# A graph layer and a 64-expert feed-forward layer on one core: node sums in rows, shared-expert pieces and the base addition earlier in the run

## The chip, the cores and the metric

The program runs on one core of a Trainium2 chip. The metric is the device time of one execution in microseconds (us), smaller is better. TensorE (PE), VectorE (DVE), ScalarE (ACT), GpSimd (POOL) and SyncE (SP) work side by side and meet at semaphores. Here SP issues the loads of weights, and POOL issues all gathers and scatters between the on-chip memory and DRAM.

## The reference, cut to what matters

```python
# x (625, 512); src, dst: 5000 edges in both directions and 625 loops, sorted by dst
h0  = layernorm(x)
agg = segment_sum(h0[src], dst, 625)
h   = (1 + eps) * h0 + agg
h   = relu(batch_norm(h @ W1 + b1)); h = relu(batch_norm(h @ W2 + b2))
x   = x + h0 + h
xn  = layernorm(x)
gate = the 6 best of softmax(xn @ Wr) over 64 experts, rescaled to sum 1
out = x + xn + sum over 2 shared experts of ffn(xn) + sum over 64 experts of ffn_e(xn) * gate[:, e]
# ffn: (silu(x @ Wg) * (x @ Wu)) @ Wd, all matrices 512 x 512, float32
```

## The kernel before, in words

**The graph part.** The 625 nodes are T = 5 blocks of P = 125. The sum over edges is a product with the matrix A that counts edges from each source node to each destination node. A is made block by block of destinations: each block has GB = 5 groups of 25 destinations, and each group has U = 5 chunks of edges. For each group DVE makes two arrays of ones and zeros, 125x625 each, by comparing a constant with a column: `one_s` (source) and `one_m` (destination and source block) in `group_onehots` (L697 to L702). PE multiplies them (`visit`, L1097, five matmuls) and ACT copies the block's product from PSUM into `aT` (`at_copy`, L484 and L486). DVE adds (1 + eps) to the diagonal of `aT` (`at_diag`, L761). Then PE aggregates (`aggregate`, L1110): for each of 4 column quarters and 5 source blocks one matmul with `h0` as the stationary operand and `aT` as the moving one, 20 matmuls of 125 columns in float32. What comes out is h transposed, and ACT copies it to `hT` (L497). On PE the order is visits(0), visits(1), aggregate(0), visits(2), aggregate(1), and so on. Two products with weights and batch norms follow (L1172 and L1185), then layer norm and routing, until about 165 us.

**The expert part.** It is one loop over j = 0 to 63 (L1425 to L1467 on PE). The experts are sorted by how many rows they have; the table ROWS says how many rows are worked for the j-th: 96 for j up to 5, 64, 60, 56 and 52 for j = 6 to 46, 96 and 80 for j = 47 to 62. Below, j = 6 to 46 are the light rounds. One round of PE does, in this order: the gate product of j, the transposes of the hidden rows of j-1 (`ident,hs`), the transposes of the gathered rows of j+1 (`ident,xg`, L1355), a small product for the slots of j+3 (L1270), the up product of j, in some rounds a piece of the shared experts, and the down product of j-1. Where an expert has 96 rows, up comes right after gate (`gate_and_up`, L1379). X(j) is the time at which PE transposes the rows of j.

**The pieces.** The two shared experts are 26 pieces: per expert 8 for gate and up (L1325 and L1335 each half of one) and 5 for down (L1346, 8 matmuls, added to `x_sb` by DVE). Three are done ahead of the loop or at j = 0, and 23 are spread evenly over j = 6 to 46 by the table `unit_at` (L310 to L313).

**POOL's order.** POOL executes gather(j), then scatter(j-5), for j = 0 to 68. A gather reads rows of `x_tab` into one of three `xg` buffers (L424). A scatter adds expert j's rows in `ysb` to `out` in DRAM (L436). Scatters are one behind another: each waits until the one before has landed, and there are three `ysb` buffers, which ACT fills (L623). After scatter 47 (`BASE_AFTER`) POOL issues the base: two transfers that add `x_sb` to `out` (L446). They wait for all ten down pieces and for scatter 47. Scatter 48 waits for the base.

**The ring.** SP loads each expert's three matrices (1 MB each) in the order of use into 13 slots. A load waits for the last product that read its slot, and the core's other transfers share the DMA engines with them.

Of the kernel before, what the change touches and what calls it, by code (L numbers as in the profile page):

```python
# [21 lines left out]
def gnn_moe_kernel(nc, x_in, src_in, dst_in, eps_in, W1, b1, g1, be1, W2, b2, g2, be2,  # L22
# [42 lines left out]
    BASE_AFTER = 47  # L65
    NY = 3
    PRE = 3 * 16
# [4 lines left out]
    with ctx:  # L72
# [58 lines left out]
        iota_m = m("iota_m", [P, P], i16)  # L131
# [33 lines left out]
        aT = [rAT.place(f"aT{i}", [P, T, P], f32) for i in range(2)]  # L165
# [43 lines left out]
        ring = [rOh.place(f"ring{i}", [128, KD, 512], f32) for i in range(8)]  # L209
# [31 lines left out]
        def sem(name):  # L241
# [14 lines left out]
        s_vecT, s_sm, s_vis, s_atc, s_at, s_h0, s_nrm, s_xs = (sem(n) for n in (  # L256
            "vectors_T", "group_onehots", "group_visited", "aT_copied", "aT_ready", "h0_ready", "norm_ready", "extra_round"))
        s_agg, s_hT, s_hpad = (sem(n) for n in ("aggregated", "hT_ready", "hT_padded"))
# [56 lines left out]
        assert max(unit_at) < BASE_AFTER  # L315

# [4 lines left out]
        def _(sp):  # L321
# [54 lines left out]
        def _(pool):  # L376
# [13 lines left out]
            g.iota(iota_m[:], pattern=[[1000, T], [1, G]], base=1000, channel_multiplier=0).then_inc(s_cst, 1)  # L390
# [83 lines left out]
        def _(act):  # L474
# [20 lines left out]
            def agg_copy(b):  # L495
                act.wait_ge(s_agg, b + 1)
                sc.activation(hT[:, :, b * P:(b + 1) * P],  # L497
                              ps[:, 4 + b % 2, 0:KD * P].rearrange("p (k n) -> p k n", k=KD), ACT.Copy).then_inc(s_hT, 1)

            block_copy(0)  # L500
# [3 lines left out]
            for t in range(T):  # L504
                sc.activation(h0[:, t, :], x_sb[:, t, :], ACT.Identity, bias=negm[:, t:t + 1],
                              scale=rstd[0:P, t:t + 1]).then_inc(s_h0, 1)
            act.wait_ge(s_pre, PRE)
            block_copy(1)
            for b in range(2, T):
                agg_copy(b - 2)  # L510
                block_copy(b)
            agg_copy(T - 2)
            agg_copy(T - 1)
            act.wait_ge(s_round, 1)
            more_rounds = act.value_load(rounds_i[0:1, 0:1], min_val=0, max_val=XROUNDS)
            with act.If(more_rounds > 0):
                with act.Fori(0, more_rounds) as o:
                    for b in range(T):
                        act.wait_ge(s_vis, o * NG + (NG + GB * (b + 1)))
                        act.wait_ge(s_agg, o * T + (T + b))  # L520
                        at_copy(b, 0, 0)
# [9 lines left out]
            act.wait_ge(s_at, T)  # L531
# [125 lines left out]
        def _(dve):  # L657
# [39 lines left out]
            def group_onehots(g, slot):  # L697
                c = slice(g * U, (g + 1) * U)
                for one, iota, col in ((one_s, iota_s, col_s), (one_m, iota_m, col_m)):
                    last = v.tensor_tensor(one[slot][:], iota[:].unsqueeze(1).broadcast_to([P, U, P]),  # L700
                                           col[:, c].unsqueeze(2).broadcast_to([P, U, P]), ALU.is_equal)
                last.then_inc(s_sm, 1)  # L702

            def block_onehots(b, first=0, end=GB):
                for g in range(b * GB + first, b * GB + end):
                    if g >= NSM:
                        dve.wait_ge(s_vis, g - NSM + 1)
                    group_onehots(g, g % NSM)

            dve.wait_ge(s_col, 1)  # L710
            link(columns())
# [45 lines left out]
            def at_diag(b):  # L757

                dve.wait_ge(s_atc, 2 * b + 2)
                sl = aT[b % 2][:, b, :]  # L760
                v.scalar_tensor_tensor(sl, ident[0:P, 0:P], eps1[:], sl, ALU.mult, ALU.add).then_inc(s_at, 1)  # L761

            dve.wait_ge(s_pre, PRE)
            v.memset(hT[:, :, N:NP], 0.0).then_inc(s_hpad, 1)
            for b in range(1, T):
                block_onehots(b, 0, 2)
                at_diag(b - 1)
                block_onehots(b, 2, GB)
            at_diag(T - 1)
            dve.wait_ge(s_round, 1)  # L770
            more_rounds = dve.value_load(rounds_i[0:1, 0:1], min_val=0, max_val=XROUNDS)
            with dve.If(more_rounds > 0):
                with dve.Fori(0, more_rounds) as o:
# [6 lines left out]
                    for b in range(T):  # L780
                        dve.wait_ge(s_vis, o * NG + (NG + GB * b))
                        for i in range(GB):
                            group_onehots(b * GB + i, i)
                        dve.wait_ge(s_agg, o * T + (T + b + 1))
                        block = hT[:, :, b * P:(b + 1) * P]
                        v.tensor_tensor(block, block, ps[:, 4, 0:KD * P].rearrange("p (k n) -> p k n", k=KD),
                                        ALU.add).then_inc(s_hT, 1)
# [295 lines left out]
        def _(pe):  # L1083
# [26 lines left out]
            def aggregate(from_aT, bank):  # L1110
                for d in range(KD):
                    for s in range(T):
                        last = t_.matmul(ps[:, bank, d * P:(d + 1) * P], h0[:, s, d * 128:(d + 1) * 128],
                                         from_aT[:, s, :], start=(s == 0), stop=(s == T - 1))
                last.then_inc(s_agg, 1)

            def block_aggregate(b):
                pe.wait_ge(s_at, b + 1)
                if b == 0:
                    pe.wait_ge(s_h0, T)  # L1120
                if b >= 2:
                    pe.wait_ge(s_hT, b - 1)
                aggregate(aT[b % 2], 4 + b % 2)
# [391 lines left out]
```

## Time and profile before

| | |
|---|---|
| Median of 3 runs | 772.82 us (771.66 to 773.99) |
| The profiled execution | 773.9 us, span 772.2 us |
| Mean granted TensorE clock | 0.987 |
| Busy: PE, DVE, ACT, POOL | 714.7, 260.2, 196.8, 171.7 us |
| Moved by DMA | 236.34 MB, 306 GB/s on average |

The durations used below are those of the profiled execution. Its span leaves out 1.7 us at the ends. PE is busy 93% of the span, so first one asks which stretches of PE could be shorter, and then where PE stands idle.

### The profile page before, as it was taken

The numbers are of one execution on the slowest core, as the hardware profiler recorded it, in microseconds if no ns is written. First come the engines' busy times: TensorE is split into PE (matmuls) and PEld (weight loads), VectorE is DVE, ScalarE is ACT, GpSimd is POOL, SyncE is SP. The second block draws the span as 40 slices with busy tenths as digits, with TensorE's granted clock in tenths as the row PEclk, the third lists the DMA queues.
The fourth block names the chain that finished last, engine by engine and source line by source line (L and its number), as shares of the span: only waits on it lengthen the run. The fifth ranks groups of instructions, "written<-read, shape, count | busy, mean of one in ns | idle before, by whom it ended". The sixth has DMA issues, their size and how long they took to land. (4 is left out here: it accounts for less than half of the span.)

```text
span 772.2 us, 17458 instructions
## 1 busy us (share of the span) xinstructions
PE 714.7 (93%) x7096; PEld 485.1 (63%) x7096; DVE 260.2 (34%) x788; ACT 196.8 (25%) x497; POOL 171.7 (22%) x157
## 2 busy tenths in 40 slices
PE   2599999879999999999999999999999996999991
PEld 2597777556776666555566666655557774777760
DVE  7982624976112442222212212122332221222110
ACT  1222422311332222221122222212112331333331
POOL 4000000011222222232232213222333312222222
PEclk9999999999999999999999999999999998999997
DMA  8970020434999999999999999999999999999951
GB/s 259 407 296 3 0 109 21 169 113 158 371 359 349 350 379 392 395 385 391 373 390 386 380 388 384 393 384 386 382 388 380 374 358 344 373 371 371 371 137 24
DMA packets 57264, 236.34 MB, mean 306 GB/s; under 512 B 6171, under 2 KB 6335, under 8 KB 40286
## 3 DMA queue, kind: packets, MB, share of 16 engines
q1 hardware_dynamic: 46004, 211.33, 71.4%
q0 software_dynamic: 10144, 20.56, 11.4%
q10 hardware_dynamic: 1034, 3.30, 1.1%
q8 instruction: 59, 0.97, 0.5%
q14 instruction: 23, 0.19, 0.1%
HBM read 222.32 MB, written 12.83 MB: 305 GB/s over the span
## 5 line engine op out<-in xcount | busy, mean ns | idle before, releaser
L1362 PE MATMUL ps<-ring,xT 128*64 128x256 f32 x1296 | 153.6, 382 | 0.0
L424 POOL DMA_INDIRECT xg<-x_tab,idx_sb x64 | 68.9, 1076 | 368.0 <-DVE idx_sb L937 201.9
L436 POOL DMA_INDIRECT out<-ysb,idx_sb x64 | 92.5, 1445 | 217.5 <-issue 180.2
L1362 PEld LDWEIGHTS ps<-ring,xT 128*64 128x64 f32 x1296 | 91.1, 137 | 44.3 <-issue 1.6
L930 DVE TENSOR_REDUCE gates<-ps 128x1 f32<-128x3 f32 (+1 forms) x62 | 10.0, 162 | 285.8 <-PE ps L1270 277.4
L623 ACT ACTIVATE ysb<-ps 64x256 f32<-64x256 f32 x64 | 24.2, 378 | 260.6 <-PE ps L1362 211.3
L1362 PE MATMUL ps<-ring,hTj 128*64 128x256 f32 x624 | 76.3, 387 | 0.0
L1362 PE MATMUL ps<-w,xT 128*64 128x256 f32 x608 | 71.9, 381 | 0.0
L898 DVE TENSOR_TENSOR onehot<-iotaAB,slotv 125x640 bf16<-125x640 f32 (+1 forms) x64 | 67.3, 1051 | 1.4 <-PE ps L1278 1.0
L1362 PEld LDWEIGHTS ps<-ring,hTj 128*64 128x64 f32 x624 | 42.5, 138 | 30.5 <-issue 12.6
L1362 PEld LDWEIGHTS ps<-w,xT 128*64 128x64 f32 x608 | 42.5, 137 | 20.4
L994 DVE SCALAR_TENSOR_TENSOR hs<-hs,gates,ps 128x256 f32<-128x256 f32 x64 | 30.7, 480 | 59.8 <-PE ps L1362 41.9
L613 ACT ACTIVATE hs<-ps 128x256 f32<-128x256 f32 (+1 forms) x64 | 26.9, 421 | 91.3 <-PE ps L1369 52.1
L1362 PE MATMUL ps<-w,hTj 128*64 128x256 f32 x320 | 38.6, 383 | 2.1 <-ACT hTj L617 2.1
L1325 PE MATMUL ps<-xnT,sw 128*128 128x312 f32 (+1 forms) x128 | 37.9, 438 | 0.4 <-ACT lg L566 0.4
L1346 PE MATMUL ps<-sw,hsT 128*125 128x512 f32 x80 | 37.0, 605 | 0.0
L1335 PE MATMUL ps<-xnT,sw 128*128 128x312 f32 (+1 forms) x128 | 36.5, 427 | 0.0
L1355 PE MATMUL ps<-ident,xg 96*128 96x96 f32 (+5 forms) x256 | 30.1, 239 | 6.8 <-DMA xg<-x_tab,idx_sb 6.8
L1172 PE MATMUL ps<-hT,w 128*128 128x313 f32 x128 | 34.1, 427 | 1.7 <-issue 1.7
L1185 PE MATMUL ps<-r,w 128*128 128x313 f32 x128 | 34.1, 426 | 0.0
L1362 PEld LDWEIGHTS ps<-w,hTj 128*64 128x64 f32 x320 | 22.0, 137 | 16.2 <-issue 6.7
L1355 PEld LDWEIGHTS ps<-ident,xg 96*128 96x128 f32 (+5 forms) x256 | 22.6, 140 | 14.5 <-DMA xg<-x_tab,idx_sb 7.5
(237 smaller groups left out, 820.9 us busy)
## 6 DMA issues: line engine op xcount, KB each, us to landing
ring<-in_L_ffn_Wg SPq DMA_DIRECT2D x41, 1024.0 KB
ring<-in_L_ffn_Wu SPq DMA_DIRECT2D x40, 1024.0 KB
ring<-in_L_ffn_Wd SPq DMA_DIRECT2D x39, 1024.0 KB
w<-in_L_ffn_Wd SPq DMA_DIRECT2D x20, 1024.0 KB
w<-in_L_ffn_Wg SPq DMA_DIRECT2D x19, 1024.0 KB
w<-in_L_ffn_Wu SPq DMA_DIRECT2D x19, 1024.0 KB
ring_x<-in_L_ffn_Wu SPq DMA_DIRECT2D x5, 1024.0 KB
ring_x<-in_L_ffn_Wd SPq DMA_DIRECT2D x5, 1024.0 KB
```

Source lines behind the costliest of these rows:

```text
L424: g.indirect_dma_start(out=xg[j % NX][0:ROWS[j], :], out_offset=None, in_=x_tab, in_offset=bass.IndirectOffsetOnAxis(ap=idx_sb[0:ROWS[j], ...
L436: g.indirect_dma_start(out=out, out_offset=bass.IndirectOffsetOnAxis(ap=idx_sb[0:ROWS[j], j:j + 1].bitcast(u32), axis=0), in_=ysb[j % NY][ ...
L613: sc.activation(o, i, ACT.Silu).then_inc(s_silu, 1)
L898: v.tensor_tensor(onehot[e % 2][:].rearrange("p t a c -> p t (a c)")[:, :, 0:n], iotaAB[0:P, :, :].rearrange("p a c -> p (a c)")[:, 0:n].u ...
L994: last = v.scalar_tensor_tensor(o, o, ga, u, ALU.mult, ALU.mult)
L1172: last = t_.matmul(ps[:, q + h, 0:HALF], w1[buf][:, k, col:col + 128], halves(hT, k)[h], start=(k == 0), stop=(k == KD - 1))
L1185: last = t_.matmul(ps[:, q + h, 0:HALF], w2[k // KD][:, k % KD, col:col + 128], halves(r1, k)[h], start=(k == 0), stop=(k == KH - 1))
L1325: last = t_.matmul(ps[:, 5, 0:PART[h]], sw[0][:, k, f * 128:(f + 1) * 128], xnT[:, k, c0:c0 + PART[h]], start=(k == 0), stop=(k == KD - 1))
L1335: last = t_.matmul(ps[:, 6, 0:PART[h]], sw[1][:, k, f * 128:(f + 1) * 128], xnT[:, k, c0:c0 + PART[h]], start=(k == 0), stop=(k == KD - 1))
L1346: last = t_.matmul(ps[0:P, 5, :], hsT[:, k, t * P:(t + 1) * P], sw[2][:, k, :], start=(k == 0), stop=(k == KD - 1))
L1355: last = t_.transpose(ps[:, 4, k * rows:(k + 1) * rows], xg[h][0:rows, k * 128:(k + 1) * 128], ident[0:rows, 0:rows])
L1362: last = t_.matmul(ps[h * BIG:(h + 1) * BIG, bank, 0:AW], big(k), w[:, k, h * AW:(h + 1) * AW], start=(k == 0), stop=(k == KD - 1))
```

## The change

- **Compares.** ACT writes the column of a group out to its full width (`rep`, 125x625 in int16, ten buffers), and DVE compares two 2-byte arrays of full width. This is done for `one_m` in all 25 groups, and for `one_s` in the last five. 30 ACT instructions are added.
- **Aggregation.** It now gives rows: `aT` is the stationary operand and h0 the moving one, 512 columns wide. As `aT` and h0 are read in the type f32r, h0 is split into a rounded part `h0_hi` (5 more ACT instructions) and the rest `h0_lo` (5 subtractions on DVE): 10 matmuls per block in place of 20. DVE adds (1 + eps) h0 on the way out of PSUM (`h_rows`, 125x512, in place of `at_diag`), and PE transposes the rows (4 per block). Block b is aggregated right after its own visits; the transposes come one block later.
- **Last block.** DVE adds it into `hT`, where ACT copied before.
- **Memory.** The new arrays lie where ring slots 4 to 7 are, so SP loads those slots only after `hT` is done.
- **Gate and up** are adjacent for all experts from j = 1.
- **Pieces.** The 23 pieces are spread over j = 6 to 34 (the last is at 33, and runs after X(34)).
- **Base.** It follows scatter 36, and from there on POOL issues gather(j+1) ahead of scatter(j-5), where it was gather(j).

The diff, cut to its core:

```diff
-    BASE_AFTER = 47
+    BASE_AFTER = 36
+    NREP = 10
...
-        free = [j for j in range(FIXED, FIXED + E - LAST - NBIG) if j not in (SPREAD + 4, SPREAD + 5)]
+        free = [j for j in range(FIXED, 35) if j not in (SPREAD + 4, SPREAD + 5)]
...
             for i, (r, j) in enumerate(items):
+                if i == 4:
+                    sp.wait_ge(s_hT, T)
...
             for j in range(E + LAG):
-                if j < E:
+                if j < E and j <= BASE_AFTER + LAG + 1:
                     gather(j)
                 if j >= LAG:
+                    if BASE_AFTER + LAG + 1 < j + 1 < E:
+                        gather(j + 1)
                     scatter(j - LAG)
                 if j == BASE_AFTER + LAG:
                     add_base()
...
+                    sc.activation(rep[n % NREP][:], col[:, g * U:(g + 1) * U].unsqueeze(2).broadcast_to([P, U, P]),
+                                  ACT.Copy).then_inc(s_rep, 1)
...
             for b in range(2, T):
-                agg_copy(b - 2)
+                if b + 1 < T:
+                    spread(b + 1)
                 block_copy(b)
...
+            def h_rows(b):
+                dve.wait_ge(s_agg, b + 1)
...
+                v.scalar_tensor_tensor(hrow[b % 2][:], h0[:, b, :], eps1[:], ps[0:P, 4 + b % 2, :], ALU.mult,
+                                       ALU.add).then_inc(s_hrow, 1)
...
-            def aggregate(from_aT, bank):
-                for d in range(KD):
-                    for s in range(T):
-                        last = t_.matmul(ps[:, bank, d * P:(d + 1) * P], h0[:, s, d * 128:(d + 1) * 128],
-                                         from_aT[:, s, :], start=(s == 0), stop=(s == T - 1))
+            def aggregate(from_aT, bank, done):
+                for s in range(T):
+                    for part in (h0_hi, h0_lo):
+                        last = t_.matmul(ps[0:P, bank, :], from_aT[:, s, :], part[:, s, :],
+                                         start=(s == 0 and part is h0_hi), stop=(s == T - 1 and part is h0_lo))
...
+            block_aggregate(0)
+            block_aggregate(1)
             for b in range(2, T):
-                block_aggregate(b - 2)
+                if b == T - 1:
+                    block_transposes(b - 2)
                 visits(b)
+                block_transposes(b - 1 if b == T - 1 else b - 2)
+                block_aggregate(b)
...
-                both = j >= 1 and CAPS[j] > BIG
+                both = j >= 1
```

**POOL around the base.** A name with `ysb` is a scatter, one with `xg` a gather, one with `x_sb` half of the base. Before:

```order
L436 DMA out<-ysb_149,idx_sb 625x512
L446 DMA out<-x_sb 112x5x512
L446 DMA out<-x_sb 13x5x512
L424 DMA xg_141<-x_tab,idx_sb 80x512
L436 DMA out<-ysb_147,idx_sb 625x512
L424 DMA xg_139<-x_tab,idx_sb 80x512
L436 DMA out<-ysb_148,idx_sb 625x512
```

and in the change, where the first row is scatter 36:

```order
L457 DMA out<-ysb_150,idx_sb 625x512
L467 DMA out<-x_sb 112x5x512
L467 DMA out<-x_sb 13x5x512
L445 DMA xg_142<-x_tab,idx_sb 52x512
L445 DMA xg_143<-x_tab,idx_sb 52x512
L457 DMA out<-ysb_151,idx_sb 625x512
L445 DMA xg_144<-x_tab,idx_sb 52x512
L457 DMA out<-ysb_152,idx_sb 625x512
```

The gathers behind the base are now of 52 rows, gather 42 is still right behind it, and gather 43 has moved ahead of scatter 37.

**ACT in the graph part.** `aT` rows are the copies of a block of A, `rep` rows the spreads, `hT` rows the copies of h transposed. Before, for blocks 3 and 4:

```order
L484 ACTIVATE aT_101<-ps 125x4x5x25
L486 ACTIVATE aT_101<-ps 125x5x25
L497 ACTIVATE hT<-ps 128x4x125
L484 ACTIVATE aT_100<-ps 125x4x5x25
L486 ACTIVATE aT_100<-ps 125x5x25
```

and in the change, from block 2's copies to those of block 3:

```order
L507 ACTIVATE aT_99<-ps 125x4x5x25
L509 ACTIVATE aT_99<-ps 125x5x25
L520 ACTIVATE hT<-ps 128x4x125
L530 ACTIVATE rep_104<-col_s 125x625
L530 ACTIVATE rep_168<-col_m 125x625
L530 ACTIVATE rep_169<-col_s 125x625
L530 ACTIVATE rep_170<-col_m 125x625
L530 ACTIVATE rep_171<-col_s 125x625
L530 ACTIVATE rep_172<-col_m 125x625
L530 ACTIVATE rep_173<-col_s 125x625
L530 ACTIVATE rep_174<-col_m 125x625
L530 ACTIVATE rep_175<-col_s 125x625
```

One more `rep` row follows, and then block 3's copies: all ten spreads of the last block stand ahead of them.

**PE in the light rounds.** A round runs from one `ident,xg` row to the next; `xT` rows are gate or up, `hTj` rows down, and `xnT,sw` rows a piece. Before, one whole round with a gate and up piece, from X(34) to X(35):

```order
L1355 MATMUL ps<-ident,xg_140 128x56 x4
L1270 MATMUL ps<-gsel_89,onehot_174 128x5 x5
L1362 MATMUL ps<-w_0_118,xT_143 64x256 x8
L1325 MATMUL ps<-xnT,sw_165 128x312 x4
L1335 MATMUL ps<-xnT,sw_166 128x312 x4
L1362 MATMUL ps<-w_1_119,hTj 64x256 x8
L1362 MATMUL ps<-w_0_163,xT_142 64x256 x8
L1395 MATMUL ps<-ident,hs_145 128x128 x2
L1355 MATMUL ps<-ident,xg_141 128x56 x4
```

and in the change two rounds, the last piece (`hsT`, a down piece) in the first of them:

```order
L1449 MATMUL ps<-ident,xg_143 128x56 x4
L1364 MATMUL ps<-gsel_88,onehot_188 128x5 x5
L1440 MATMUL ps<-sw_181,hsT 125x512 x4
L1456 MATMUL ps<-w_1_122,hTj 64x256 x8
L1456 MATMUL ps<-w_0_177,xT_145 64x256 x8
L1456 MATMUL ps<-w_1_178,xT_145 64x256 x8
L1493 MATMUL ps<-ident,hs_148 128x128 x2
L1449 MATMUL ps<-ident,xg_144 128x56 x4
L1364 MATMUL ps<-gsel_89,onehot_189 128x5 x5
L1456 MATMUL ps<-ring_x,hTj 64x256 x8
L1456 MATMUL ps<-ring_158,xT_146 64x256 x8
L1456 MATMUL ps<-ring_159,xT_146 64x256 x8
```

Gate and up have come together, and from the second round on, up to j = 46, no round has a piece.

## Rows read from the trace of the kernel before

**Rows 1.** The page: busy time, granted clock in tenths and GB/s in 40 slices.
```profile
PE 714.7 (93%) x7096; PEld 485.1 (63%) x7096; DVE 260.2 (34%) x788; ACT 196.8 (25%) x497; POOL 171.7 (22%) x157
...
GB/s 259 407 296 3 0 109 21 169 113 158 371 359 349 350 379 392 395 385 391 373 390 386 380 388 384 393 384 386 382 388 380 374 358 344 373 371 371 371 137 24
```

**Rows 2.** Timeline of PE, graph part: start us, us, instructions, [idle before <-releaser].
```profile
31.09 7.00 PE L1113 MATMUL ps<-aT,h 125*128 125x125 f32 x40 [0.18 <-issue]
37.92 1.61 PE L1100 MATMUL ps<-one_m,one_s 125*125 125x125 bf16 x25
39.37 4.68 PE L1113 MATMUL ps<-aT,h 125*128 125x125 f32 x40
...
63.71 34.05 PE L1172 MATMUL ps<-hT,w 128*128 128x313 f32 x128 [1.67 <-issue]
```

**Rows 3.** Timeline of DVE, graph part.
```profile
9.16 0.81 DVE L700 TENSOR_TENSOR one_s<-iota_s,col_s 125x625 bf16<-125x625 int16 x1
9.89 0.81 DVE L700 TENSOR_TENSOR one_m<-iota_m,col_m 125x625 bf16<-125x625 int16 x1
...
22.52 0.81 DVE L700 TENSOR_TENSOR one_s<-iota_s,col_s 125x625 bf16<-125x625 int16 x1
...
51.69 0.81 DVE L700 TENSOR_TENSOR one_m<-iota_m,col_m 125x625 bf16<-125x625 int16 x1
```

**Rows 4.** Timeline of ACT, graph part.
```profile
22.34 3.64 ACT L505 ACTIVATE h<-x_sb,negm,rstd 125x512 f32<-125x512 f32 x5 [1.26 <-DVE negm L751]
...
53.09 0.60 ACT L484 ACTIVATE aT<-ps 125x500 f32<-125x500 f32 x1 [2.35 <-PE ps L1100]
53.58 0.27 ACT L486 ACTIVATE aT<-ps 125x125 f32<-125x125 f32 x1
```

**Rows 5.** Groups of instructions by line and shape: busy us, mean ns of one, idle before.
```profile
L952 DVE COPY scratch<-scratch 128x42 f32<-128x42 f32 x1 | 0.2, 185 | 0.0
L952 DVE COPY scratch<-scratch 128x22 f32<-128x22 f32 x1 | 0.2, 178 | 0.0
...
L1346 PE MATMUL ps<-sw,hsT 128*125 128x512 f32 x80 | 37.0, 605 | 0.0
L1016 DVE TENSOR_TENSOR x_sb<-x_sb,ps 125x512 f32<-125x512 f32 x10 | 6.9, 688 | 30.6 <-PE ps L1346 30.6
```

**Rows 6.** Timeline of PE at X(6), X(33), X(34), X(35), X(53) and X(63).
```profile
225.92 0.46 PE L1355 MATMUL ps<-ident,xg 64*128 64x64 f32 x4
...
461.79 0.45 PE L1355 MATMUL ps<-ident,xg 56*128 56x56 f32 x4
...
468.09 0.46 PE L1355 MATMUL ps<-ident,xg 56*128 56x56 f32 x4
...
478.94 0.45 PE L1355 MATMUL ps<-ident,xg 56*128 56x56 f32 x4
...
645.75 0.79 PE L1355 MATMUL ps<-ident,xg 80*128 80x80 f32 x4 [6.55 <-DMA xg<-x_tab,idx_sb]
...
743.28 0.45 PE L1355 MATMUL ps<-ident,xg 52*128 52x52 f32 x4
```

**Rows 7.** Timeline of POOL around the base: scatter 47, base, gather 53, scatter 48.
```profile
616.25 1.46 POOL L436 DMA_INDIRECT out<-ysb,idx_sb  x1 [2.47 <-issue]
625.65 2.53 POOL L446 DMA_DIRECT2D out<-x_sb  x2 [7.94 <-DMA out<-ysb,idx_sb]
628.48 1.02 POOL L424 DMA_INDIRECT xg<-x_tab,idx_sb  x1 [0.30 <-issue]
645.60 1.52 POOL L436 DMA_INDIRECT out<-ysb,idx_sb  x1 [16.10 <-DMA out<-x_sb]
```

**Rows 8.** Timeline of POOL: scatters in the light rounds, the last after X(33).
```profile
353.98 1.45 POOL L436 DMA_INDIRECT out<-ysb,idx_sb  x1 [5.46 <-issue]
...
362.07 1.45 POOL L436 DMA_INDIRECT out<-ysb,idx_sb  x1 [3.46 <-issue]
...
464.84 1.45 POOL L436 DMA_INDIRECT out<-ysb,idx_sb  x1 [0.30 <-issue]
```

**Rows 9.** Waits: who waited for what, us in total, times, longest.
```profile
ACT ysb L623 <- DMA out<-ysb,idx_sb: 43.2, 10, 7.2
```

**Rows 10.** Windows: length, busy us (x) of PE, PEld, DVE, ACT, POOL, granted clock, DMA share, GB/s.
```profile
300.00:400.00 100.00, 100.00 (x750) 58.88 (x746) 21.50 (x62) 23.00 (x62) 28.23 (x23) 1.00 1.03 387
```

More of the change, by code:

```diff
@@ L164, in gnn_moe_kernel @@
         ring_x = rH0.place("ring_x", [128, KD, 512], f32)
-        aT = [rAT.place(f"aT{i}", [P, T, P], f32) for i in range(2)]
+        aT = [rAT.place(f"aT{i}", [P, T, P], f32r) for i in range(2)]
+        iota_m = rAT.place("iota_m", [P, U, P], i16)
+        hrow = [rAT.place(f"hrow{i}", [P, D], f32) for i in range(2)]
+        rep = [rAT.place("rep0", [P, U, P], i16)]
         rAT.rewind()
@@ L208, in gnn_moe_kernel @@
         cntS = rWin.place("cntS", [128, E], f32)
-        ring = [rOh.place(f"ring{i}", [128, KD, 512], f32) for i in range(8)]
+        ring = [rOh.place(f"ring{i}", [128, KD, 512], f32) for i in range(4)]
+        upper = rOh.at
+        ring += [rOh.place(f"ring{4 + i}", [128, KD, 512], f32) for i in range(4)]
+        past = rOh.at
+        rOh.at = upper
+        h0_hi = rOh.place("h0_hi", [P, T, D], f32r)
+        h0_lo = rOh.place("h0_lo", [P, T, D], f32r)
+        rep += [rOh.place(f"rep{i}", [P, U, P], i16) for i in range(1, NREP)]
+        assert rOh.at <= past
+        rOh.at = past
         w2 = [rOh.place(f"w2_{i}", [128, KD, 512], f32) for i in range(2)]
@@ L315, in gnn_moe_kernel @@
         assert max(unit_at) < BASE_AFTER
+        BOTH_FROM = NG - GB
+        spreads = [(g, c) for g in range(NG) for c in (("s", "m") if g >= BOTH_FROM else ("m",))]
+        spread_at = {gc: n for n, gc in enumerate(spreads)}
         block = ctx.enter_context(nc.Block())
@@ L493, in block_copy, with hT_copy, spread @@
                 at_copy(b, b % 2, 2 * (b % 2))
-            def agg_copy(b):
-                act.wait_ge(s_agg, b + 1)
+            def hT_copy(b):
+                act.wait_ge(s_hrT, b + 1)
                 sc.activation(hT[:, :, b * P:(b + 1) * P],
-                              ps[:, 4 + b % 2, 0:KD * P].rearrange("p (k n) -> p k n", k=KD), ACT.Copy).then_inc(s_hT, 1)
+                              ps[:, 6 + b % 2, 0:KD * P].rearrange("p (k n) -> p k n", k=KD), ACT.Copy).then_inc(s_hT, 1)
+            def spread(b):
+                for n, (g, c) in enumerate(spreads):
+                    if g // GB != b:
+                        continue
+                    if n >= NREP:
+                        act.wait_ge(s_sm, spreads[n - NREP][0] + 1)
+                    col = col_m if c == "m" else col_s
+                    sc.activation(rep[n % NREP][:], col[:, g * U:(g + 1) * U].unsqueeze(2).broadcast_to([P, U, P]),
+                                  ACT.Copy).then_inc(s_rep, 1)
+            act.wait_ge(s_colm, 1)
+            spread(0)
+            spread(1)
             block_copy(0)
@@ L695, in columns, with group_onehots @@
                 return v.tensor_tensor(col_m[:], ps[0:P, 6, 256:256 + NV], grp_of[:], ALU.subtract)
[L697 removed]
+            def group_onehots(g, slot, spread):
                 c = slice(g * U, (g + 1) * U)
[L699 to L701 removed]
+                if spread and g >= BOTH_FROM:
+                    v.tensor_tensor(one_s[slot][:], iota_s[:].unsqueeze(1).broadcast_to([P, U, P]),
+                                    rep[spread_at[g, "s"] % NREP][:], ALU.is_equal)
+                else:
+                    v.tensor_tensor(one_s[slot][:], iota_s[:].unsqueeze(1).broadcast_to([P, U, P]),
+                                    col_s[:, c].unsqueeze(2).broadcast_to([P, U, P]), ALU.is_equal)
+                if spread:
+                    last = v.tensor_tensor(one_m[slot][:], iota_m[:], rep[spread_at[g, "m"] % NREP][:], ALU.is_equal)
+                else:
+                    last = v.tensor_tensor(one_m[slot][:], iota_m[:], col_m[:, c].unsqueeze(2).broadcast_to([P, U, P]),
+                                           ALU.is_equal)
                 last.then_inc(s_sm, 1)
@@ L755, in _ @@
             link(v.tensor_scalar(eps1[:], ps[0:P, 7, 300:301], 1.0, None, ALU.add))
[L757 to L761, printed above, removed]
-            dve.wait_ge(s_pre, PRE)
[L764 to L769, printed above, removed]
+            def h_rows(b):
+                dve.wait_ge(s_agg, b + 1)
+                if b >= 2:
+                    dve.wait_ge(s_hrT, b - 1)
+                v.scalar_tensor_tensor(hrow[b % 2][:], h0[:, b, :], eps1[:], ps[0:P, 4 + b % 2, :], ALU.mult,
+                                       ALU.add).then_inc(s_hrow, 1)
+            block_onehots(1)
+            for t in range(T):
+                dve.wait_ge(s_hi, t + 1)
+                dve.wait_ge(s_h0, t + 1)
+                v.tensor_tensor(h0_lo[:, t, :], h0[:, t, :], h0_hi[:, t, :].bitcast(f32), ALU.subtract).then_inc(s_lo, 1)
+            block_onehots(2, 0, 4)
+            h_rows(0)
+            block_onehots(2, 4, GB)
+            block_onehots(3, 0, 2)
+            h_rows(1)
+            block_onehots(3, 2, GB)
+            h_rows(2)
+            block_onehots(4, 0, 4)
+            h_rows(3)
+            block_onehots(4, 4, GB)
+            dve.wait_ge(s_pre, PRE)
+            v.memset(hT[:, :, (T - 1) * P:NP], 0.0).then_inc(s_hadd, 1)
+            h_rows(T - 1)
             dve.wait_ge(s_round, 1)
```

103 lines of the change are left out of this document (69 added, 34 removed).

## The prediction

> **What bounds the kernel now.** I read the page first. PE is busy 714.7 of 772.2 us, while DMA runs at 359 to 396 GB/s in nearly every slice from 190 us on [rows 1]: two resources are close to full side by side. So the question for each stretch is which of the two gives the pace, and whether a shift of PE work makes the other one late. Then the timelines. In the graph part PE waits for the compares of DVE, one after another without a gap, and the first weight product starts at 63.71 us [rows 2, 3]. In the expert part between 300 and 400 us PE is busy 100% with the clock at 1.00 and 387 GB/s [rows 10]. PE's only long idle time there is before X(53), 6.55 us for a gather [rows 6].
>
> Of this kernel's measurement, about 0.3% (2.3 us) can be told from no change. The profiled execution took 773.9 us, 1.1 above the median of 772.8; I sum against 773.9 and take 1.1 off at the end.
>
> **The graph part.** Prices first.
> - A compare is issued every 0.72 us (9.16 to 9.89) [rows 3]. With two full 2-byte inputs its price isn't in the trace. Upper end: 0.72, nothing gained. Lower end: DVE's cheapest rate per element here, 7 ns for 20 elements (185 - 178 ns) [rows 5], so 625 cost 0.22 us. I take 0.45, the middle, as no row is nearer to either end. The Trainium skill, page "VectorE: DVE Perf Modes", section "The perf-mode tier table", says that a two-input operation on 16-bit data in SBUF runs at twice the rate of a float32 one; by it a compare would take about 0.37 us, an estimate from the page, and the graph part would end at most 1 us earlier.
> - A matmul of aggregation is 512 columns in a rounding type. Upper end: the 80 records of the 512-column float32 product are 37.0 us, two records each, so 0.93 us [rows 5]. Lower end: bf16, 1.61 us for 25 matmuls of 125 columns [rows 2], so 0.26 us for 512. I take 0.25, as a type that rounds its operand is nearer to bf16; 10 of them are 2.5 us against half of 9.15, 4.6 us, or 4.68 for 40 records, for a block now [rows 2]. The Trainium skill, page "FP8 and Floating Point Precision", section "TensorE Precision Notes", gives four passes for true float32 and a reduced-precision read of the same bytes; no row of this trace shows that read, and with four passes a block would cost 9.3 us.
> - A spread on ACT, one input of 625: a scaling of 512 is issued every 0.71 us (3.64 / 5, with overlap) [rows 4]; I take 0.65.
> - `h_rows` and the last add on DVE: 0.69 us like the add out of PSUM [rows 5]. A subtraction for `h0_lo`: 0.6.
>
> The path, block by block. DVE starts at 9.16 [rows 3]; with a wait for the first spread it is 9.9. Block 0 takes 5 x (0.72 + 0.45) = 5.8, to 15.7. The statistics between blocks 0 and 1 keep their 6.1 us (9.16 + 10 x 0.72 = 16.4 to 22.52) [rows 3]; block 1 is done at 27.7. ACT scales h0 twice, 10 x 0.71 from 21.7, to 28.8; `h0_lo` is done at 30.7. Then groups 10 to 19 (11.7 us) and three `h_rows` take DVE to 44.3. Here a new wait comes: **ACT has all ten spreads of the last block ahead of block 3's copies.** They can start only as their buffers come free, from group 10's compare on, and end at 46.8. So block 3's copy, for which PE is ready at about 44.2, ends at 47.7, its aggregation at 50.2, `h_rows` at 51.0, and the last group's compares at 51.9 (this last one is at 52.5 now, so DVE's gain is nearly gone). Visit 0.5, copy 0.9 (0.60 and 0.27) [rows 4], aggregation 2.5, `h_rows` 0.7, transposes 0.6 and add 0.7 lead to 57.8; with the 1.0 from there to the first weight product, it starts at 58.8 instead of 63.7. **-4.9 us.** What gives most of it is the end of the chain: the last two aggregations, 9.15 us [rows 2], are now one of 2.5. PE stands idle for some 3 us before block 3's copy. Bounds: -8 (no wait for the spreads, compares 0.37) to +1 (compares 0.72, and a clock that falls in the gaps). The ring loads that must wait for `hT` are issued at 58 and are used after 165: nothing.
>
> **The pieces.** Between X(34) and X(35) a round with a gate and up piece takes 478.94 - 468.09 = 10.85 us, and the one before, without a piece, 6.30 [rows 6]. So a gate and up piece is 4.55, and a down piece 37.0 / 10 = 3.7, with its hand-over 3.78. By the tables, 11 gate and up and 5 down pieces lie between X(6) and X(35) now, and 13 and 10 after the change. So X(35) comes 2 x 4.55 + 5 x 3.78 = **28.0 us later**, and what is left behind X(35) is 28.0 us shorter on PE alone. If PE were the only bound, that is nothing. DMA says otherwise: 12 rounds without a piece take PE 75.6 us; in these the ring wants 3.15 MB an expert, and gather, scatter and base more. So the light rounds run at what the transfers give.
>
> **The scatters.** A scatter follows the landing of the one before. In the light rounds they are issued 362.07 - 353.98 = 8.1 us apart [rows 8], while PE's rounds there average 8.7 with pieces (253.0 / 29 between X(6) and X(35)) [rows 6]; ACT waits ten times, up to 7.2 us, for a `ysb` buffer whose scatter isn't landed [rows 9]. With rounds of 6.3 PE outruns them. Scatter 30 is issued 3.05 after X(33) (464.84 - 461.79) [rows 6, 8], so scatter 32 at X(35)+3.05 and scatter 36 at X(35)+3.05+4 x 8.1 = +35.4. The base is issued 625.65 - 616.25 = 9.4 later [rows 7], +44.8. The gather behind it lets PE start 645.75 - 625.65 = 20.1 after the base [rows 6, 7]: X(42) = X(35)+64.9. PE's own pace is 7 x 6.3 = 44.1. **Stall +20.8 us**, where the stall now, before X(53), is 6.55 and with the rest of that round 7.4 over its neighbours: **-7.4**. The gather that runs ahead doesn't help at 42: gather 42 is itself behind the base.
>
> After the stall scatter 37 starts only when the base has landed, 20 after it, and PE is two scatters ahead. The third `ysb` buffer lets one round through, and the next four light ones go at 8.1 instead of 6.3: **+7.2**. From X(48) on rounds are of 9.4 and scatters keep up.
>
> The Trainium skill, page "DMA: Bandwidth & Descriptors", section "Queues, rings and completion order", says that each DMA engine takes turns between the queues it has work for. The trace agrees: gather 53, issued at 628.48 behind the base in POOL's own queue, lets PE go 17.3 us later, while the ring's loads went on.
>
> **Gate and up adjacent.** The same products in another order; in the 96-row rounds it is so already and PE has no gap. Nothing, bounds -2 to +3 (if up waits for DVE's product of the round before).
>
> **Sum.** 773.9 - 4.9 + 28.0 - 28.0 - 7.4 + 20.8 + 7.2 = 789.6, less 1.1: **788 us**.
>
> **The rivals.**
> - *The scatters keep up with light rounds (chance 0.20).* For it: near the end scatters with less beside them follow faster, and the spacing of 8.1 was seen with PE slower than that, so it isn't proved to be a limit. Against: those ten waits of ACT. Then scatter 36 is at X(39)+3.05, base at +12.4, X(42) at X(39)+32.5 instead of +18.9: a stall of 13.6 and no slow rounds after. 773.9 - 4.9 - 7.4 + 13.6 - 1.1 = 774 us, about no change.
> - *The base is cheap where it stands now (0.14): faster.* 20.1 us are for a base that competes with ring loads of 96-row rounds; should the ring be full, with PE stalled or ahead, the base lands in the time of a usual gather, 6.5 us after its issue, and hides in X(39) to X(42). It decides if base and gather together take under 9 us. Then no stall: 773.9 - 4.9 - 7.4 - 1.1 = 760.5, and up to 2 more: 762 us. Against it: DMA is near 390 GB/s throughout [rows 1], and light rounds want most.
> - *The graph part gains nothing (0.10).* Compares stay at 0.72, or the wait for the spreads is longer: the first weight product at 63.7 or later, 788.5 + 5 = 794 us. With four passes in the aggregation it would be beyond the range.
> - That gate and up come together and nothing else moves is sure from the order; there is no rival of that kind.
>
> **How the numbers follow.** Forecast 0.56, the rivals 0.20, 0.14 and 0.10. The forecast's own range is 780 to 797: stall 16 to 25, slow rounds 4 to 10, graph part -8 to -2. The range for 8 in 10 takes in the first rival and the third: **768 to 799**. It leaves out most of the second rival and the four passes. Faster by over 0.3%: the second rival, and a third of the first, with 0.01 of the forecast: 0.22. Within 0.3%: 0.07 of the first and 0.03: 0.10. Slower: 0.68.
>
> **What would show it.** The first weight product at 57 to 61 us, with ten spreads in a row on ACT ahead of block 3's copies. X(35) at 478.9 + 28.0 - 4.9, near 502. Between X(35) and X(42) scatters 8 us apart; then an idle PE before X(42), 15 to 25 us, released by the gather behind the base; ACT waiting for scatters in the rounds 43 to 47; no stall before X(53). I am wrong if scatters follow at 6.3 us, if PE's longest idle time there is under 10 us, or if X(35) isn't 28 us later against the first weight product.

## The result, and the profile after

The changed kernel takes 791.89 us (median of 4 runs, 791.55 to 793.06), the kernel before 773.34 beside it. The ratio is 1.024, with a 95% interval of 1.022 to 1.026: slower by 18.6 us. The profiled execution has a span of 791.3 us, against 772.2.

The page of the changed kernel, busy time and GB/s in 40 slices [rows 1]:

```profile
PE 707.0 (89%) x6966; PEld 477.9 (60%) x6966; DVE 252.6 (32%) x794; ACT 217.5 (27%) x531; POOL 173.4 (22%) x157
...
GB/s 279 410 41 211 106 1 106 127 129 263 365 371 350 312 385 383 387 393 392 387 390 336 351 385 357 357 382 393 303 341 383 381 374 371 375 367 376 273 34 20
```

PE has 7.7 us less to do and the program is 19.1 us longer. The slices 22 and 23 (336 and 351 GB/s), 25 and 26 (357) and 29 and 30 (303 and 341) move less than the slices before did [rows 1].

The graph part, timeline of PE [rows 2]:

```profile
40.20 0.39 PE L1189 MATMUL ps<-h_lo,aT 125*125 125x512 f32 x1
40.44 0.39 PE L1189 MATMUL ps<-h_hi,aT 125*125 125x512 f32 x1
...
47.10 0.50 PE L1189 MATMUL ps<-h_hi,aT 125*125 125x512 f32 x1 [2.76 <-ACT aT L509]
...
57.71 14.53 PE L1266 MATMUL ps<-hT,w 128*128 128x313 f32 x54 [0.84 <-DVE hT L862]
```

of DVE [rows 3]:

```profile
9.61 0.82 DVE L747 TENSOR_TENSOR one_s<-iota_s,col_s 125x625 bf16<-125x625 int16 x1 [0.89 <-POOL gid L434]
10.34 0.48 DVE L750 TENSOR_TENSOR one_m<-iota_m,rep 125x625 bf16<-125x625 int16 x1
10.73 0.81 DVE L747 TENSOR_TENSOR one_s<-iota_s,col_s 125x625 bf16<-125x625 int16 x1
```

and of ACT [rows 4]:

```profile
45.07 0.72 ACT L530 ACTIVATE rep<-col_s 125x625 int16<-125x625 f32 x1
45.68 0.72 ACT L530 ACTIVATE rep<-col_m 125x625 int16<-125x625 f32 x1
46.29 0.59 ACT L507 ACTIVATE aT<-ps 125x500 fp32r<-125x500 f32 x1
```

A compare with two 2-byte inputs is issued 0.39 us before the next (10.34 to 10.73), an aggregation matmul 0.24 us (40.20 to 40.44), a spread 0.61 us (45.07 to 45.68). Block 3's copy starts right behind the tenth spread, and PE stands idle for it, 2.76 us. The first weight product starts at 57.71 where it was at 63.71.

The expert part, timeline of PE at X(6), X(34), X(35), X(41), X(42), X(43) and X(63) [rows 6]:

```profile
221.13 0.46 PE L1449 MATMUL ps<-ident,xg 64*128 64x64 f32 x4
...
488.48 0.46 PE L1449 MATMUL ps<-ident,xg 56*128 56x56 f32 x4
...
498.31 0.45 PE L1449 MATMUL ps<-ident,xg 56*128 56x56 f32 x4
...
536.62 0.45 PE L1449 MATMUL ps<-ident,xg 52*128 52x52 f32 x4 [0.46 <-DMA xg<-x_tab,idx_sb]
...
568.61 0.67 PE L1449 MATMUL ps<-ident,xg 52*128 52x52 f32 x4 [25.62 <-DMA xg<-x_tab,idx_sb]
...
577.86 0.45 PE L1449 MATMUL ps<-ident,xg 52*128 52x52 f32 x4
...
762.61 0.39 PE L1449 MATMUL ps<-ident,xg 52*128 52x52 f32 x3
```

and of POOL around the base: scatter 36, base, gathers 42 and 43, scatter 37 [rows 7]:

```profile
536.06 1.45 POOL L457 DMA_INDIRECT out<-ysb,idx_sb  x1 [5.50 <-issue]
545.35 2.51 POOL L467 DMA_DIRECT2D out<-x_sb  x2 [7.84 <-DMA out<-ysb,idx_sb]
548.16 1.01 POOL L445 DMA_INDIRECT xg<-x_tab,idx_sb  x1 [0.30 <-issue]
549.48 0.96 POOL L445 DMA_INDIRECT xg<-x_tab,idx_sb  x1 [0.30 <-issue]
567.91 1.50 POOL L457 DMA_INDIRECT out<-ysb,idx_sb  x1 [17.48 <-DMA out<-x_sb]
```

PE waits 25.62 us for gather 42, which lands 23.3 us after the base behind which it stands. From X(6) to X(35) it takes 277.2 us (253.0 before), from X(35) to X(63) 264.3, the same as before to 0.1 us although seven pieces have left this stretch.

### The profile page after: what moved, and what is told of

It is laid out like the page before. It is cut to its first block, busy times and chain, and to the rows that moved or that the text cites. A ratio compares the mean times of both kernels' runs of the same rounds, so it can differ in the third digit from the quotient of the medians.

```text
span 791.3 us, 17266 instructions
## 1 busy us (share of the span) xinstructions
PE 707.0 (89%) x6966; PEld 477.9 (60%) x6966; DVE 252.6 (32%) x794; ACT 217.5 (27%) x531; POOL 173.4 (22%) x157
## 4 chain that ended last, share of the span: by engine, by line
PE 71%; DMA 10%; issue 9%; DVE 6%; ACT 2%; POOL 1%; POOLq 0%; ACTq 0%; DVEq 0%
PE ps L1456 33%; DMA out<-ysb,idx_sb 8%; PE ps L1463 8%; PE ps L1440 4%; PE ps L1266 4%; PE ps L1279 4%; PE ps L1419 4%; PE ps L1429 4%; DMA out<-x_sb 3%; PE ps L1493 3%; PE ps L1449 2%; PE ps L1189 2%; PE ps L1364 1%; DVE one_s L747 1%; ACT rep L530 1%
## 5 line engine op out<-in xcount | busy, mean ns | idle before, releaser
L1456 PE MATMUL ps<-ring,xT 128*64 128x256 f32 x1296 | 149.6, 382 | 0.0
L1456 PEld LDWEIGHTS ps<-ring,xT 128*64 128x64 f32 x1296 | 94.6, 138 | 47.1 <-issue 2.3
L1456 PE MATMUL ps<-ring,hTj 128*64 128x256 f32 x624 | 79.2, 398 | 4.9 <-ACT hTj L661 4.9
L1456 PEld LDWEIGHTS ps<-w,xT 128*64 128x64 f32 x608 | 44.8, 139 | 22.2 <-issue 1.3
L661 ACT ACTIVATE hTj<-ps 128x256 f32<-128x256 f32 (+1 forms) x64 | 26.8, 419 | 74.6 <-PE ps L1493 74.6
L1456 PE MATMUL ps<-w,hTj 128*64 128x256 f32 x320 | 40.6, 397 | 2.6 <-ACT hTj L661 2.1
L1070 DVE SCALAR_TENSOR_TENSOR hs<-hs,gates,ps 128x256 f32<-128x256 f32 x64 | 30.5, 476 | 28.9 <-PE ps L1463 16.4
```

Source lines behind the costliest of these rows:

```text
L1070: last = v.scalar_tensor_tensor(o, o, ga, u, ALU.mult, ALU.mult)
L1456: last = t_.matmul(ps[h * BIG:(h + 1) * BIG, bank, 0:AW], big(k), w[:, k, h * AW:(h + 1) * AW], start=(k == 0), stop=(k == KD - 1))
```

## The experiments

Each of them was timed beside the kernel before (medians 772.8 to 773.4 us).

**e1: the changed kernel, only the base back at 47.**

```diff
-    BASE_AFTER = 36
+    BASE_AFTER = 47
```

> The changed kernel with the base back behind scatter 47; the pieces stay early. Theory (rounds without pieces run at the scatters' pace, and the base costs a stall wherever it stands): no stall before X(42); X(35) to X(47) takes 88 to 94 us instead of 75.6, since PE runs out of ysb buffers, then a stall of 7 to 15 us before X(53). Median 772 to 780. Rival (scatters keep up with light rounds): X(35) to X(47) takes 76 to 78 us, the median is 760 to 766. Rival (the early base is what costs, at this place and no other): the median falls by the whole 25 us stall, to 767.

788.37 us, ratio 1.020 (1.017 to 1.023): 8 us above the theory's range, and over 20 above both rivals. X(35) to X(47) takes 91.1 us, as the theory had it, and the stall is 17.0, 2 above its range. PE is at X(47) 6.7 us later than before, and the stall is 10.5 us longer than before: these two make nearly the whole loss, and the range for the median was too low for them. Timeline of PE at X(35), X(47), X(53):

```profile
498.18 0.39 PE L1449 MATMUL ps<-ident,xg 56*128 56x56 f32 x3
...
589.30 0.39 PE L1449 MATMUL ps<-ident,xg 96*128 96x96 f32 x2 [1.68 <-DMA xg<-x_tab,idx_sb]
...
663.52 0.80 PE L1449 MATMUL ps<-ident,xg 80*128 80x80 f32 x4 [17.02 <-DMA xg<-x_tab,idx_sb]
```

PE is further ahead of the scatters when the base comes (scatter 47 is issued 44.4 us after X(47), before 33.6), so it waits 17 us and not 7. The base at 36 costs only 3.5 us more than at 47: **the place of the base is not what makes the change slow.**

**e2: e1, and the pieces over 6 to 46 again.** What is left of the change is the graph part, the adjacency and the gather that runs ahead.

```diff
-        free = [j for j in range(FIXED, 35) if j not in (SPREAD + 4, SPREAD + 5)]
+        free = [j for j in range(FIXED, FIXED + E - LAST - NBIG) if j not in (SPREAD + 4, SPREAD + 5)]
```

> The changed kernel with the base behind scatter 47 and the pieces over j = 6 to 46 as before; the graph part, the adjacent gate and up, and the gather that runs ahead stay. Theory: the losses are all in pieces and base; what is left is the graph part (-6.0) and 0.23 us for each piece that no longer stands between gate and up (23 pieces, -5.4): median 761 to 764. Rival (DMA bounds the whole expert part, so PE's gain comes back as a longer stall at X(53)): 766 to 771.

768.32 us, ratio 0.994 (0.992 to 0.996). It is above the theory's range and in the rival's, and the rival's sign is there too: at X(48) PE is 11.5 us ahead of the kernel before, at X(53) only 4.9, as the stall before X(53) has grown from 6.55 to 12.5 us. Timeline of PE at X(53):

```profile
640.89 0.79 PE L1449 MATMUL ps<-ident,xg 80*128 80x80 f32 x4 [12.50 <-DMA xg<-x_tab,idx_sb]
```

Whether DMA's volume or the chain of scatters makes this stall is left to e9 and e10. Against e1 one table differs, and 20.1 us: **the early pieces are the loss.**

**e3: the changed kernel without a base.** The two transfers and the waits for them are left out, so `out` lacks x_sb.

> The changed kernel without the base: the two transfers that add x_sb to out, and the waits for them, are left out, so the output lacks x_sb. The pieces stay early. Theory: the 25.5 us stall before X(42) goes, but the light rounds after X(42) are then held by scatters up to X(47): X(35) to X(47) takes 88 to 94 us. Median 768 to 774, less by the transfers' 7 us than the kernel with the base at 47. Rival (scatters keep up): X(35) to X(47) 76 to 78 us, median 758 to 761.

778.32 us, ratio 1.007 (1.005 to 1.009), above the range. X(35) to X(47) takes 91.8 us. There is no long stall, and X(63) is at 738.1, but the end comes 39.4 us later and not 28.9. The scatters explain little of that: the last one is issued 24.0 us after X(63), before 21.7. The rest stands behind it: from its issue to the end are 15.4 us, before 7.3, and from 766 us on the trace shows no instruction and no transfer. What ends there isn't shown. So e3 shows that the light rounds take as long without a base; its median, with these 8 us in it, is no price of the base.

**e4: the kernel before, only gate and up adjacent.**

```diff
...
-                both = j >= 1 and CAPS[j] > BIG
+                both = j >= 1
```

> The kernel before with gate and up adjacent and nothing else. Theory: each of the 23 rounds with a piece is 0.23 us shorter, rounds without one stay at 6.30: median 767 to 768.5. Rival (DMA sets the pace, and the time comes back before X(53)): 771 to 773, with the stall before X(53) longer by what the rounds gained.

773.52 us, ratio 1.001 (0.999 to 1.002): the rival was right, if 0.5 us above its range. Rounds with a piece are 0.24 us shorter (10.61 for 10.85) and X(47) is 4.4 us earlier, but POOL's timeline, scatter 47 and the base, reads

```profile
616.57 1.46 POOL L436 DMA_INDIRECT out<-ysb,idx_sb  x1 [6.89 <-issue]
626.35 2.53 POOL L446 DMA_DIRECT2D out<-x_sb  x2 [8.32 <-DMA out<-ysb,idx_sb]
```

where it was 616.25 and 625.65 [rows 7]. PE became faster, the chain of scatters did not, and PE's 13.6 us before X(53) give the time back.

**e5: e2 with the base behind scatter 58; e6: the kernel before with the base behind scatter 58.**

> The kernel e2_spread46 with the base behind scatter 58 in place of 47, where in e2 the scatters land in 3.9 to 5 us because the ring's loads are over. Theory (the base costs 17 to 25 us only where ring loads share the DMA engines, and it stops the chain of scatters for that time): no stall before X(53), the base and its gap take 5 to 9 us in the chain's end, PE is at X(63) 10 to 14 us earlier, and the end is 8 to 14 us earlier: median 754 to 761. Rival (the scatters are the bound in the 96-row rounds too, at 9.0 to 9.5 each): the stall goes but the lag of the scatters comes back at the end, median 762 to 768. Rival (DMA volume is the bound): 766 to 770.

766.83 us, ratio 0.990 (0.986 to 0.994): where the two rivals overlap, above the theory, and no better than e2 by more than its spread.

> The kernel before with the base behind scatter 58, nothing else. Theory: the stall of 7.4 us before X(53) goes, the base costs 2 to 5 us in the last scatters: median 766 to 771. Rival (scatters bound): 771 to 774.

772.74 us, ratio 0.999 (0.998 to 1.001), the rival. In e6 PE is at X(63) 10.3 us earlier, and the end is only 1.4 earlier. Timeline of POOL at the end of e6:

```profile
729.51 1.54 POOL L446 DMA_DIRECT2D out<-x_sb  x1 [7.71 <-DMA out<-ysb,idx_sb]
731.43 0.94 POOL L446 DMA_DIRECT2D out<-x_sb  x1 [0.38 <-issue]
744.59 1.53 POOL L436 DMA_INDIRECT out<-ysb,idx_sb  x1 [12.22 <-issue]
```

Scatter 59 follows the base by 15.1 us, which take the place of the stall.

**e7: e2 without the adjacency**, so the graph part with pieces and base as before.

```diff
-                both = j >= 1
+                both = j >= 1 and CAPS[j] > BIG
```

> The kernel before with the change's graph part and its gather ahead behind scatter 47, without adjacent gate and up; pieces and base as before. After e4 gave nothing, theory: this carries the whole gain of e2, median 767 to 769. Rival (the graph part's 6 us is given back at X(53) as the adjacency's was): 771 to 773.

766.24 us, ratio 0.992 (0.989 to 0.995), a little below the theory's range. Against the kernel before e7 gains 7.2 us, and the gain is carried to the end. Not all of it is the graph part's: the first weight product starts 6.4 us earlier (57.30), and the step from X(1) to X(2), the same products in all kernels, takes 13.89 us where it was 15.45. The granted clock in this step was 1.00, before 0.89.

**e8: the changed kernel with gathers 42 and 43 ahead of the base.**

```diff
...
                 if j == BASE_AFTER + LAG:
+                    gather(j + 1)
+                    gather(j + 2)
                     add_base()
```

> The changed kernel with gathers 42 and 43 issued ahead of the base and not behind it. Theory (the base holds scatter 37 and through the three ysb buffers PE; the gather is only the first wait to show): the stall before X(42) goes, but PE stops within X(43) to X(45) for 15 to 22 us, released by ACT's wait for scatter 37: median 784 to 790. Rival (the gather behind the base is the cost): the 25 us go, median 766 to 772.

790.91 us, ratio 1.022 (1.018 to 1.025), a little above the theory's range and far from the rival. The wait before X(42) falls from 25.62 to 3.61 us, and X(44) is at 584.30, in the changed kernel at 584.15. Timeline of PE, X(43) and what comes after:

```profile
554.21 0.45 PE L1451 MATMUL ps<-ident,xg 52*128 52x52 f32 x4
554.60 0.28 PE L1366 MATMUL ps<-gsel,onehot 125*128 125x5 bf16 x5
576.67 3.68 PE L1458 MATMUL ps<-w,hTj 128*64 128x256 f32 x16 [21.80 <-ACT hTj L663]
```

and in the table of waits

```profile
ACT ysb L669 <- DMA out<-ysb,idx_sb: 151.3, 24, 27.7
```

ACT stands 27.7 us in front of a `ysb` buffer, and behind it stands the copy of the hidden rows for which PE waits. The gather is the wait that shows first; the held scatter is the one that costs.

**e9 and e10: two chains.** Odd experts add to a second array in DRAM, each scatter waits for the one before in its own chain; `out` lacks the odd experts. The base and the `ysb` buffers wait for both chains. e9 is e1 with this, e10 is e2 with this.

```diff
-                if j >= 1:
-                    pool.wait_ge(s_scat, 16 * j)
+                if j >= 2:
+                    pool.wait_ge((s_scat, s_scat_b)[j % 2], 16 * (j // 2))
...
-                g.indirect_dma_start(out=out,
+                g.indirect_dma_start(out=(out, out_b)[j % 2],
```

> The kernel e1_base47 (pieces early, base behind scatter 47) with two chains of scatters: even experts add to out, odd ones to a second DRAM array, and each waits only for its own chain; the output lacks the odd experts. Base and buffers wait for both chains. Theory (the serial chain of scatters, 8 to 9 us a link, is what holds the light rounds): X(35) to X(47) falls from 91.1 us to 76 to 80, ACT's waits for scatters fall from 126 us to under 30, the stall before X(53) from 17.2 to under 10 us, median 768 to 776. Rival (DMA volume holds them: the core moves 385 GB/s there whatever the order): X(35) to X(47) may shorten by what the ring had stored, but PE then waits for ring loads and the median stays within 4 us of e1's 788.

767.18 us, ratio 0.992 (0.989 to 0.995): 21.2 us below e1, and a little below the theory's range.

> The kernel e2_spread46 (pieces over 6 to 46) with the same two chains; the output lacks the odd experts. Theory (chain): the stall before X(53), 12.7 us for the gather there, falls to 7 or less, since the base is issued with PE and not 8 us behind it; median 758 to 763. Rival (DMA volume): 766 to 769.

756.54 us, ratio 0.978 (0.974 to 0.983): 11.8 us below e2, also below the theory's range. The stall before X(53) is 5.2 us, in e2 12.5: it was the chain's. Timeline of PE in e9 at X(35), X(47), X(53):

```profile
495.58 0.39 PE L1463 MATMUL ps<-ident,xg 56*128 56x56 f32 x3
...
577.68 0.41 PE L1463 MATMUL ps<-ident,xg 96*128 96x96 f32 x3
...
641.86 0.66 PE L1463 MATMUL ps<-ident,xg 80*128 80x80 f32 x3 [5.22 <-DMA xg<-x_tab,idx_sb]
```

and ACT's waits for scatters, in e1 first:

```profile
ACT ysb L667 <- DMA out<-ysb,idx_sb: 125.7, 22, 7.1
```

```profile
ACT ysb L681 <- DMA out<-ysb,idx_sb: 7.6, 2, 5.8
...
ACT ysb L681 <- DMA out_b<-ysb,idx_sb: 5.9, 2, 3.0
```

The same bytes move in this stretch, and 82.1 us do what took 91.1; the 76 to 80 expected aren't reached. **The serial chain of scatters holds the light rounds.** Of the 21.2 and 11.8 us, 2.9 and 1.6 are again the step from X(1) to X(2): 13.89 us at a clock of 1.00 in e9 and e10, 16.80 at 0.82 in e1, 15.45 at 0.89 in e2. That leaves the reading as it is. But e9 is still 10.6 us above e10: with the single chain gone, the early pieces cost half as much, by something else. The windows of the stretch with packed pieces point to it (length, busy us of five engines, clock, DMA share, GB/s), before and then the changed kernel:

```profile
400.00:490.00 90.00, 90.00 (x700) 57.82 (x699) 19.56 (x60) 21.11 (x56) 25.17 (x21) 1.00 1.03 385
```

```profile
400.00:490.00 90.00, 90.00 (x643) 54.74 (x642) 18.68 (x57) 19.44 (x51) 21.53 (x18) 1.00 0.98 362
```

With rounds of 9.8 to 10.6 us PE frees ring slots more slowly than DMA could fill them, and 23 GB/s over 90 us are 2.1 MB, 5.4 us at 385 GB/s, for this window alone. Bytes not moved there have to be moved later. In e9 PE waits eleven times for ring loads between 555 and 594 us, 7.9 us in all, and in e10 not once there. Two of e9's waits:

```profile
558.07 1.95 PE L1470 MATMUL ps<-ring,xT 128*64 128x256 f32 x16 [1.07 <-DMA ring<-in_L_ffn_Wu]
...
564.08 1.95 PE L1470 MATMUL ps<-ring,xT 128*64 128x256 f32 x16 [1.10 <-DMA ring<-in_L_ffn_Wg]
```

and the windows of e9 and then e10 in these 39 us, PE busy 31.3 and 38.9, with 385 and 382 GB/s:

```profile
555.00:594.00 39.00, 31.32 (x340) 21.26 (x342) 10.39 (x27) 8.35 (x22) 14.43 (x10) 1.00 1.03 385
```

```profile
555.00:594.00 39.00, 38.94 (x483) 27.27 (x483) 13.34 (x33) 10.31 (x28) 15.16 (x10) 1.00 1.03 382
```

So the ring's loads are a second bound close behind the chain. In e1 and in the changed kernel PE doesn't wait for the ring in the light rounds behind X(35), as the chain holds it back first.

**e11: e7 with six of the last ten spreads behind block 3's copies.**

```diff
...
-                    spread(b + 1)
+                    spread(b + 1, 0, 2 if b + 1 == T - 1 else GB)
                 block_copy(b)
+                if b + 1 == T - 1:
+                    spread(T - 1, 2, GB)
```

> The kernel e7_front_only with six of the last block's ten spreads behind block 3's copies on ACT. Theory: block 3's copy ends at 44.9 instead of 46.9 us, the last DVE compares at 49 instead of 51.3, and the first weight product starts 1.5 to 2.5 us earlier; median 764 to 766 (e7: 766.2). Rival (the last spreads now come late to DVE): no earlier start, 766 to 767.5.

The first weight product starts at 55.54 for 57.30, as expected, but the median is 767.38 (764.39 to 770.42), ratio 0.992 (0.988 to 0.995): above the theory's range, and no difference from e7 that can be told. At X(6) the profiled e11 is later than e7 (218.95 and 217.84), as X(1) to X(2) took 16.77 and 13.89 us. The traces tell what that step is: it takes 13.89 us where the granted clock was 1.00 (e7, e9, e10), 15.45 at 0.89 (before, e2) and 16.8 at 0.82 (the changed kernel, e1, e11). In the 7.1 us before it PE was busy 4.5 us in each of these. So why the clock fell in one and not in another stays open, and so does whether it belongs to the kernel or to the single execution.

**e12: a whole version with two chains.** The base goes into the second array's chain, the second array is read back and added to `out` at the very end. The ACT order is that of e11, and gather 54 is ahead of the base.

> A whole version with two chains: front, adjacency and pieces as in e2, the ACT order of e11; odd experts up to 57 add to a second array, the base goes into that array's chain behind scatter 47 (issued after scatter 48) and no longer stops the chain of out, gather 54 is ahead of the base, and after the last scatter the second array, read back in the meantime, is added to out in two transfers. Theory: no stall over 4 us before X(53) or X(54), so PE is at X(63) at 719 to 724; the last addition costs 5 to 9 us behind the last scatter: median 755 to 761, under e7's 766. Rival (without the stall PE catches up with the ring and waits for loads, whose last one lands at 734 to 739 anyway): X(63) at 725 to 730, median 760 to 766.

772.95 us, ratio 0.999 (0.997 to 1.001): no gain, worse than both ranges. The stall before X(53) is gone (9.40 us for that round), and two smaller waits take its place, for ring loads and for a gather (rounds of 10.77, 14.97 and 10.91). X(63) is at 729.3, as the rival had it. The end comes 42.8 us later, where it was 28.9. Of these 13.9 us, 3.3 are the scatters' (the last is issued 25.0 us after X(63), before 21.7), as from 58 on they are all in one chain while the loads still run, and 10.6 stand behind it, where the final addition is issued at 759.4. This form of the idea doesn't pay; another division of the last scatters wasn't tried.

## Why the prediction was right, point by point

788 us was forecast and 791.9 measured, in the range of 768 to 799 and by the likeliest case. The terms, each against the profiled executions (19.1 us in all, where the sum had 15.7). They were not as good as their sum: the pieces came out 3.8 us too dear and what stands behind X(35) 7.4 too cheap, and the two errors partly cancel, which is luck.
- **Graph part, -4.9.** Measured -6.0 at the first weight product and -4.8 at X(6). The prices were 0.39 for 0.45, 0.24 for 0.25 and 0.61 for 0.65, and the wait for the ten spreads came where it was put, with 2.76 us of idle PE.
- **Pieces to X(35), +28.0.** Measured +24.2. The difference is the adjacency, costed at nothing with bounds of -2 to +3, and so outside its bounds at X(35): 0.24 us for each of the 23 pieces now there is 5.5, of which the round from X(6) to X(7) took 1.7 back (7.51, before 5.79). e4 shows that in the kernel before it is worth nothing all the same.
- **The stall, +20.8.** PE was idle 25.6, and X(35) to X(42) took 70.3 for 64.9. Scatters 32 to 36 were 8.7 us apart and not 8.1 (+2.4), and gather 42 let PE go 23.3 us after the base and not 20.1 (+3.2). Right in mechanism, too small in both terms. The other stall, before X(53), went as forecast: that round took 9.40 us for 16.76, -7.4. The first named cause, that gather 42 is behind the base, is only the nearest one (e8).
- **Slow rounds, +7.2.** X(42) to X(48) took 49.9 us, 8.5 more than 5 x 6.3 + 9.9. But the form was wrong: the rounds up to X(43), X(44) and X(45) took 9.25 and twice 6.29, the waits came in the two behind (8.16 and 11.12 us). And 3.0 of the 8.5 us are not the scatters': the clock was granted at half from 547.7 us, when PE had stood idle since 543.0, to 575.0, when it had worked again for 6.4 us, and that is in the 9.25. The sum had no term for it.
- **Nothing behind X(48) but the -7.4.** Measured -6.7 for X(48) to X(63): four rounds of 96 rows that took 3.2 us longer, the -7.4, and 2.6 less behind X(53).
- **The ring.** The prediction named it ("the light rounds run at what the transfers give") and took the price from the scatters alone. With the single chain that was enough. With two chains it is not: e9 is 26.7 us behind e10 at X(35), as the pieces are packed there, and is still 9.6 behind at X(48), with 7.3 us of waits for ring loads between.

The forecast's step "the scatters" is shown by e9: with the chain cut in two, e1 loses 21.2 us. What the sum hides is whose loss it is. It priced the early pieces at 28.0 - 28.0 and gave the loss to the stall behind the early base; but with the base back at 47 (e1) 15.5 us of the loss are still there. The chain is behind PE because the pieces are early, and the base costs about as much at either place. The first rival (scatters keep up) and the second (a cheap base) are refuted by e1, whose X(35) to X(47) takes 91.1 us, and by the 20 to 23 us from the base to the scatter behind it, at 36 and at 47 alike. The third, that the graph part gains nothing, is refuted by e7.

So the 18.6 us are made of: graph part -7.2 (e7 against before), adjacency and what is left +2.1 (e2 against e7, within the spread of both), pieces early +20.1 (e1 against e2), base early +3.5 (the change against e1). In the profiled executions -1.6, +1.6, +1.3 and 0.0 of these are the step from X(1) to X(2) at another granted clock (e11), which nothing here ties to the edits.

## What to carry to other kernels

Two resources that go at the same average pace hide each other's work only if each stretch is balanced: moving PE work out of rounds in which transfers set the pace into rounds in which PE does costs twice, as neither gets back the time in which it waited. A chain of transfers, each waiting for the landing of the last, is an engine of its own; look at the spacing of its links before you make PE faster. And when a stall is removed, ask what the thing behind it was waiting for: in e6, e8 and e12 a wait went and the end stayed within 2 us, and in e4 PE's work went and its wait grew.

## What the runs showed of the hardware

- From a scatter's issue to its landing, read where POOL waits for nothing else, it took 9.3 us for 56 rows with the ring's loads beside it (scatter 36, changed kernel), and 4.7 us for 80 rows after the loads had ended (scatter 59, e3). From the base's issue to the next scatter it was 22.6 us at scatter 36, 20.8 in e1 at 47, and 15.1 in e6 at 58.
- In the changed kernel PE stood idle from 543.0 to 568.6 us and then worked without a gap to the end of the round. Its granted clock was 1.00 up to 547.7 us, 0.50, the level of 1.2 GHz, from there to 575.0, and 1.00 again.
- A step of the same products took 13.89 us at a granted clock of 1.00, 15.45 at 0.89 and 16.8 at 0.82 (X(1) to X(2), e7, the kernel before, the changed kernel).
- The operation in the rounding type took 0.24 us for 512 columns at full clock, about the bf16 rate (1.61 us for 25 matmuls of 125 columns [rows 2], which is 0.26 us for 512), so two of them, 0.48 us, are cheap beside one float32 product of as many columns, 0.93 us [rows 5].
- A compare with both inputs in full 2-byte form was issued 0.39 us before the next, and one with a broadcast column in float32 0.72. The Trainium skill, page "VectorE: DVE Perf Modes", section "The perf-mode tier table", gives a two-input operation on 16-bit data twice the rate of one on float32 data. The trace agrees: 0.39 us is near the 0.37 that the prediction estimated from that page.
